# A fused macaron block: one more second product on split halves, and normalisation one chunk earlier in the loop

## The chip, the cores and the metric

The kernel runs on one core of one Trainium2 chip. The metric is device time in microseconds (us), the median of several runs of one program; a profiled execution gives the trace. The engines are TensorE (PE; its weight loads are PEld), VectorE (DVE), ScalarE (ACT), GpSimd (POOL) and SyncE (SP), which here only issues DMAs.

## What is computed

The input x is 8 x 1024 tokens of 128 values, and the program computes three steps on it:

```python
x = x + 0.5 * ffn(layernorm(x))      # phase 0
x = x + attention(layernorm(x))
x = x + 0.5 * ffn(layernorm(x))      # phase 1

def ffn(h):                          # 16 experts of 64, and one shared expert of 128
    scores = sigmoid(h @ Wg.T)       # choose 2 of 4 groups, then 4 of 16 experts, weights cw
    hid    = relu2(einsum('th,eih->eti', h, W1))          # relu2(r) = max(r, 0)**2
    out    = einsum('eth,te->th', einsum('eti,ehi->eth', hid, W2), cw)
    return out + relu2(h @ Ws1.T) @ Ws2.T
```

Attention is causal with one head of 128 and is not touched by the change.

## The kernel before

**Groups and chunks.** The 8192 tokens are 16 groups of 512 (`NG`), and each of the two feed-forward phases goes through all 16. The hidden width of 16 x 64 + 128 = 1152 is cut into nine chunks of 128 (`NCH`, chunks 0 to 8; chunk 8 is the shared expert). For each group and chunk four engines hand one 128x512 tile on:

1. PE, `up`: the first product, in three matmuls (L1189, L1190, L1191), since each fp32 operand is split into a high and a low half in the format fp32r: high x high, high x low, low x high.
2. DVE, `gate`: relu, times the square root of the routing weight (`wb`), from PSUM into `s_sb` (L939; L941 for chunk 8, which has no weight).
3. ACT, `square`: squares `s_sb` twice, once rounded into `g_hi` (L504) and once in full into `g_f` (L505). The trace calls these tiles `shared_r` and `shared`.
4. POOL, `lo_part`: `g_lo = g_f - g_hi` (L379).
5. PE, `down`: the second product, again three matmuls, accumulated over the chunks of the group.

A chunk listed in `WHOLE` goes another way: ACT makes only `g_f`, POOL does nothing, and `down` is one matmul instruction in plain fp32 with the unsplit weight `w2_f` (L1250). The trace shows two pieces for each such instruction.

**The order of work.** Nothing is scheduled automatically. Each engine has its own program, a loop body of two groups written out chunk by chunk, and semaphores between the engines. At step c of group g, PE issues `up` four chunks ahead (`AHEAD`), then what else is tied to this step, then `down(c)`. DVE, ACT and POOL also work on chunk c + 4 at step c; so at step 4 they handle chunk 8 of this group, at step 5 chunk 0 of the next one. All engines work in the order of their programs, and an instruction that waits holds those behind it.

**Normalisation.** Group g + 4 is normalised during group g:

- DVE computes statistics (L747) at steps 1 and 3 of the group before, and their mean and variance (L754, L758) at step 0.
- POOL computes the inverse root at step 1 (L398; the same instruction serves the routing weights of another group, and waits for their sum, L919).
- DVE's `norm_shift` (L778) computes the shift. Before the change this is at step 4, after the statistics of step 3, the first part of routing and the gate of chunk 8 (L941).
- ACT's `normalise` (L460) writes `xn`, four tiles of 128x128, two at step 5 and two at step 6, in each case ahead of that step's squares.
- PE transposes `xn` at step 7 (L1220), between the `up` and the `down` of that step. ACT copies the result at step 8.

Other side work: PE's `logits` (L1228) and `o_transpose` (L1262) at step 2 and `w_transpose` (L1236) at step 6; ACT's `x_hi_copy` at step 6, followed by POOL's `x_lo_part` (L385); ACT's `wT_copy` (L446, `wT`) at step 7, after which SP writes the routing weights to DRAM and reads them back spread over the partitions (L318, four DMAs into `wb`). The first two of them must have landed before chunk 0 of that group is gated, which is seven steps later.

The last two groups of a phase have no more groups to prepare. Groups 0 to 13 do, so the transposes of `xn` stand in 14 groups of each phase; the first four groups are prepared ahead of the loop.

Of the kernel before, what the change touches and what calls it, by code (L numbers as in the profile page):

```python
# [103 lines left out]
def macaron_kernel(nc, x, Qw, Kw, Vw, Wg, bias_corr, W1, W2, Ws1, Ws2, out):  # L104
# [13 lines left out]
    HB = 3  # L118
    RING = 6

    WHOLE = (1, 5)
    PREP = 4
    PR = 4
    PADT = 3 * TG
# [8 lines left out]
    with ExitStack() as ctx:  # L133
        def sb(name, shape, dt=F32):
            return ctx.enter_context(nc.sbuf_tensor(name, shape, dt))
# [14 lines left out]
        w2_lo = sb("w2_lo", [P, NCH, D], F32R)  # L150
        w2_f = sb("w2_f", [P, len(WHOLE), D])
        wgT = sb("wgT", [P, E])
# [118 lines left out]
        def wait(eng, s, value):  # L271

            if not (isinstance(value, int) and value <= 0):
                eng.wait_ge(s, value)
# [69 lines left out]
        def _(pool):  # L344
# [22 lines left out]
            def ffn(F):  # L367
# [6 lines left out]
                def lo_part(m, j):  # L374

                    if j % NCH in WHOLE:
                        return
# [67 lines left out]
        def _(sc):  # L445
# [21 lines left out]
            def ffn(F, phase):  # L467
# [26 lines left out]
                def oT_copy(g, u):  # L494
                    sc.wait_ge(F.down_done, NCH * (g + 1))
                    wait(sc, F.oTr_done, g)
                    copy(oT[:], o_ps[u]).then_inc(F.oT_copied, 1)

                def square(m, j):

                    sc.wait_ge(F.s_done, m + 1)
                    wait(sc, F.down_done, m + 1 - RING)
                    if j % NCH not in WHOLE:
                        nc.scalar.activation(g_hi[:, j % RING, :], s_sb[:, j % RING, :], ACT.Square)  # L504
# [52 lines left out]
                def body(i, first, last, extra):  # L557
                    for u in range(UN):
                        g = i * UN + u
                        for c in range(NCH):  # L560
                            j = u * NCH + c
                            if c == 0 and not (first and u == 0):
                                oT_copy(g - 1, 1 - u)
                            if c == 3 and not last:
                                sigmoid(g + 3, 1 - u, lg_ps)
                            if c in (5, 6) and not last:
                                for t in range((c - 5) * 2, (c - 5) * 2 + 2):
                                    normalise(F, g + PREP, t)
                            if c == 6 and not last:
                                x_hi_copy(g + 2, u)  # L570
                            if c == 7 and not last:
                                wT_copy(g + 2, wT_ps)
                            if c == 8 and not last:
                                x_copy(g + PREP, u, tr_ps)
                            if not (last and j + AHEAD >= UN * NCH):
                                square(i * (UN * NCH) + j + AHEAD, (j + AHEAD) % (UN * NCH))
                            extra(j)
# [100 lines left out]
            def weights_hi(w):  # L678
# [6 lines left out]
                elif w < 4:  # L685
                    for n, c in enumerate(WHOLE):
                        if c // 4 == w - 2:
# [27 lines left out]
        def _(v):  # L715
# [44 lines left out]
            def ffn(F, phase):  # L760
# [252 lines left out]
                def body(i, first, last, extra):  # L1013
                    for u in range(UN):
                        g = i * UN + u
                        for c in range(NCH):
                            j = u * NCH + c
                            m = i * (UN * NCH) + j
                            if j + AHEAD < UN * NCH:
                                gate(i, (c + AHEAD) % NCH, m + AHEAD, j + AHEAD, (j + AHEAD) // NCH)  # L1020
                            elif not last:
                                gate(i + 1, (c + AHEAD) % NCH, m + AHEAD, (j + AHEAD) % (UN * NCH), 0)
                            if not last:
                                if c == 0:
                                    mean(g + PREP)
                                if c == 1:
                                    stats(g + PREP + 1, range(2))
                                if c == 3:
                                    stats(g + PREP + 1, range(2, TG))
                                if c == 4:  # L1030
                                    norm_shift(g + PREP)

                                for part in ((7,), (8,), (), (), (9,), (), (), (), ())[c]:
                                    route(g + 2, u, part)
                                for part in ((), (), (), (0,), (1,), (2,), (3,), (4,), (5, 6))[c]:
                                    route(g + 3, 1 - u, part)
                            if c == 2 and not (first and u == 0):
                                residual(g - 1)
                            extra(j)
# [144 lines left out]
        def _(pe):  # L1184
# [30 lines left out]
            def ffn(F, phase):  # L1215
# [29 lines left out]
                def down(g, c, m, j, u):  # L1245
                    if c == 0:
                        wait(pe, F.oT_copied, g - 1)
                    if c in WHOLE:
                        pe.wait_ge(F.sq_done, m + 1)
                        mm(o_ps[u], w2_f[:, WHOLE.index(c), :], g_f[:, j % RING, :], start=(c == 0),  # L1250
                           stop=(c == NCH - 1)).then_inc(F.down_done, 1)
# [273 lines left out]
```

## Time and profile before

| | |
|---|---|
| median of 3 runs (lowest, highest) | 725.03 us (723.0, 725.87) |
| the profiled execution: its time, its span | 725.85 us, 724.1 us |
| mean granted TensorE clock | 0.982 of 2.4 GHz |
| PE, PEld busy | 685.7 us (95%), 522.5 us (72%) |
| DVE, ACT, POOL busy | 556.3 us (77%), 522.3 us (72%), 403.9 us (56%) |
| DMA | 78.37 MB, mean 108 GB/s |

The transposes of `xn` are 15.27 us apart in the group from 217.65 to 232.92, which is the length of a group in the loop. The span runs from the first to the last instruction; 1.75 us of the execution lie around it. Busy shares are means over phases of different kinds: the feed-forward phases are about 33 to 277 us and 469 to 721 us, attention lies between. Attention gives POOL almost nothing to do, so POOL's 56% says little about how full it is in the feed-forward loop. A matmul's recorded duration overlaps with the next one's, so the time that one costs PE is the distance from its start to the next start, or its piece in the chain that ended last.

### The profile page before, as it was taken

Reading aid. Unit: us, or ns where it says so; the run is one execution under the profiler, and the core shown is the slowest. Engines: PE = TensorE matmul, PEld = TensorE weight load, DVE = VectorE, ACT = ScalarE, POOL = GpSimd, SP = SyncE. Lnnn points to the kernel's source line nnn. Section 1 sums busy time; section 2 is a strip of 40 time slices with the busy share of each in tenths; the row PEclk is TensorE's granted clock in tenths of the full one; section 3 lists DMA queues with packets and bytes.
Section 4 is the critical chain, followed back from the end, with each engine's and each line's share of the span. In section 5 each row is a group of like instructions: output and inputs, shape, how many; then the busy total and the mean of one; then the engine's idle time right before and its main releaser. Section 6 shows DMA issues by size and latency. Waiting matters only on the chain.

```text
span 724.1 us, 14916 instructions
## 1 busy us (share of the span) xinstructions
PE 685.7 (95%) x3335; PEld 522.5 (72%) x3335; DVE 556.3 (77%) x2586; ACT 522.3 (72%) x1063; POOL 403.9 (56%) x314
## 2 busy tenths in 40 slices
PE   4689999999999997999999999989999999999997
PEld 3467777777777775777777777767777777777775
DVE  5978888788887885666666678978878888788863
ACT  4478788887788866675556667657888788887875
POOL 3377877778777763000000022147787777877874
PEclk9699999999999999999999999989999999999999
DMA  9766776566775650000000000554766777667772
GB/s 250 179 129 127 158 154 142 120 137 148 150 150 119 132 104 0 1 1 1 1 0 0 0 1 1 121 117 92 150 145 148 164 165 166 149 136 173 165 165 68
DMA packets 53525, 78.37 MB, mean 108 GB/s; under 512 B 5216, under 2 KB 19184, under 8 KB 53488
## 3 DMA queue, kind: packets, MB, share of 16 engines
q1 hardware_dynamic: 51280, 77.36, 49.4%
q10 hardware_dynamic: 2208, 0.59, 0.4%
q8 instruction: 14, 0.23, 0.1%
q14 instruction: 23, 0.19, 0.1%
HBM read 72.70 MB, written 5.24 MB: 108 GB/s over the span
## 4 chain that ended last, share of the span: by engine, by line
PE 49%; DVE 21%; ACT 14%; issue 12%; ACTq 1%; POOL 1%; DVEq 1%; DMA 1%; POOLq 0%
PE psum L1189 10%; PE psum L1191 10%; PE psum L1190 9%; PE psum L1398 6%; ACT shared L505 5%; ACT xn L460 4%; PE psum L1220 3%; PE psum L1250 3%; DVE nmax L1069 3%; PE psum L1228 3%; DVE s_sb L939 2%; DVE s_sb L941 2%; DVE bn L747 2%; PE psum L1387 2%; ACT shared L611 2%
## 5 line engine op out<-in xcount | busy, mean ns | idle before, releaser
L379 POOL TENSOR_TENSOR shared_r<-shared,shared_r 128x512 fp32r<-128x512 f32 x224 | 289.0, 1291 | 115.3 <-ACT shared L505 110.3
L939 DVE SCALAR_TENSOR_TENSOR s_sb<-psum,wb 128x512 f32<-128x512 f32 x256 | 176.2, 690 | 75.8 <-PE psum L1191 65.6
L504 ACT ACTIVATE shared_r<-s_sb 128x512 fp32r<-128x512 f32 x224 | 141.3, 631 | 83.0 <-DVE s_sb L939 74.4
L505 ACT ACTIVATE shared<-s_sb 128x512 f32<-128x512 f32 x288 | 178.3, 620 | 21.7 <-DVE s_sb L939 21.4
L1189 PE MATMUL psum<-x_hi,w_hi 128*128 128x512 f32 x288 | 139.3, 484 | 2.7 <-DVE x_sb L1095 2.3
L1191 PE MATMUL psum<-x_hi,w_lo 128*128 128x512 f32 x288 | 115.3, 401 | 0.0
L1190 PE MATMUL psum<-x_lo,w_hi 128*128 128x512 f32 x288 | 114.5, 397 | 0.0
L1189 PE MATMUL psum<-shared_r,w_hi 128*128 128x512 f32 x224 | 97.8, 437 | 0.6 <-POOL shared_r L379 0.4
L1190 PE MATMUL psum<-shared_r,w_hi 128*128 128x512 f32 x224 | 89.2, 398 | 0.0
L1191 PE MATMUL psum<-shared_r,w_lo 128*128 128x512 f32 x224 | 89.0, 398 | 0.0
L362 POOL TENSOR_TENSOR a_rstd<-a_mv,neg_half 128x8 f32<-128x8 f32 x8 | 13.1, 1637 | 116.5 <-DVE a_mv L758 116.5
L1189 PEld LDWEIGHTS psum<-x_hi,w_hi 128*128 128x128 f32 x288 | 55.1, 191 | 29.6 <-issue 11.7
L1190 PEld LDWEIGHTS psum<-x_lo,w_hi 128*128 128x128 f32 x288 | 54.9, 191 | 23.9 <-issue 14.1
L1250 PE MATMUL psum<-shared,w_f 128*128 128x512 f32 x128 | 65.3, 592 | 0.0
L611 ACT ACTIVATE shared<-psum,nmax 128x128 f32<-128x128 f32 (+3 forms) x64 | 47.5, 743 | 23.6 <-DVE nmax L1069 22.3
L1191 PEld LDWEIGHTS psum<-x_hi,w_lo 128*128 128x128 f32 x288 | 54.8, 190 | 12.8
L1069 DVE TENSOR_REDUCE nmax<-psum 128x1 f32<-128x128 f32 (+3 forms) x64 | 47.6, 753 | 19.6 <-PE psum L1378 19.5
L460 ACT ACTIVATE xn<-x_sb,shift,roots 128x128 f32 (+1 forms) x128 | 55.7, 484 | 3.0 <-DVE shift L778 3.0
L1189 PEld LDWEIGHTS psum<-shared_r,w_hi 128*128 128x128 f32 x224 | 42.8, 191 | 11.0 <-POOL shared_r L379 2.4
L1191 PEld LDWEIGHTS psum<-shared_r,w_lo 128*128 128x128 f32 x224 | 42.5, 190 | 10.1
L398 POOL TENSOR_TENSOR roots<-powers,neg_half 128x8 f32<-128x8 f32 x28 | 45.9, 1638 | 6.6 <-issue 5.2
L1190 PEld LDWEIGHTS psum<-shared_r,w_hi 128*128 128x128 f32 x224 | 42.9, 192 | 6.5 <-issue 0.4
(166 smaller groups left out, 1312.1 us busy)
## 6 DMA issues: line engine op xcount, KB each, us to landing
wb<-scratch SPq DMA_DIRECT2D x128, 512.0 KB, 8.4
out<-x_sb SPq DMA_DIRECT2D x16, 256.0 KB, 9.8
x_sb<-in_L_attn_x SPq DMA_DIRECT2D x4, 256.0 KB, 6.2
scratch<-wT SPq DMA_DIRECT2D x32, 32.0 KB, 1.9
w_raw<-in_L_ffn_W ACTq DMA_DIRECT2D x1, 512.0 KB, 5.8
w_raw<-in_L_ffn_W SPq DMA_DIRECT2D x1, 512.0 KB, 6.4
w_raw<-in_L_ffn_Ws ACTq DMA_DIRECT2D x1, 64.0 KB, 8.6
w_raw<-in_L_ffn_Ws SPq DMA_DIRECT2D x1, 64.0 KB, 6.9
```

Source lines behind the costliest of these rows:

```text
L379: nc.gpsimd.tensor_tensor(g_lo[:, j % RING, :], g_f[:, j % RING, :], g_hi[:, j % RING, :].bitcast(F32), ALU.subtract).then_inc(F.glo_done, 1)
L398: nc.gpsimd.tensor_tensor(roots[:], powers[:], neg_half[:, 0:2 * TG], ALU.pow).then_inc(F.rstd_done, 1)
L460: ins = nc.scalar.activation(xn[:, t, :], x_sb[:, bass.ds(g * TG + t, 1), :].rearrange("p t d -> p (t d)"), ACT.Identity, bias=shift[:, t: ...
L504: nc.scalar.activation(g_hi[:, j % RING, :], s_sb[:, j % RING, :], ACT.Square)
L505: nc.scalar.activation(g_f[:, j % RING, :], s_sb[:, j % RING, :], ACT.Square).then_inc(F.sq_done, 1)
L611: nc.scalar.activation(prob[:, t % PR, 0:w], sc_ps[t % 2][:, 0:w], ACT.Exp, bias=nmax[:, u, t:t + 1], accum_out=rsum[:, u, t:t + 1]).then_ ...
L939: ins = nc.vector.scalar_tensor_tensor(s_, h_, 0.0, wb[:, u, c, :], ALU.max, ALU.mult)
L1069: nc.vector.tensor_reduce(nmax[:, u, t:t + 1], sc_ps[t % 2][:, 0:(t + 1) * P], AX.X, ALU.max, negate=True).then_inc(A.max_done, 1)
L1189: mm(out_, l_hi, r_hi, start=start, stop=False)
L1190: mm(out_, l_hi, r_lo, start=False, stop=False)
L1191: return mm(out_, l_lo, r_hi, start=False, stop=stop)
L1250: mm(o_ps[u], w2_f[:, WHOLE.index(c), :], g_f[:, j % RING, :], start=(c == 0), stop=(c == NCH - 1)).then_inc(F.down_done, 1)
```

## The change

Two things are changed. `WHOLE` loses chunk 1, so that only chunk 5 takes the plain fp32 way. And DVE's `norm_shift` moves from step 4 to the end of the statistics in step 3, and ACT's four normalisations from steps 5 and 6 to steps 4 and 5.

```diff
-    WHOLE = (1, 5)
+    WHOLE = (5,)
...
-                            if c in (5, 6) and not last:
-                                for t in range((c - 5) * 2, (c - 5) * 2 + 2):
+                            if c in (4, 5) and not last:
+                                for t in range((c - 4) * 2, (c - 4) * 2 + 2):
                                     normalise(F, g + PREP, t)
                             if c == 6 and not last:
                                 x_hi_copy(g + 2, u)
...
                                 if c == 3:
                                     stats(g + PREP + 1, range(2, TG))
-                                if c == 4:
                                     norm_shift(g + PREP)
```

On ACT, steps 4 to 7 of a group before the change: squares of chunk 8 (L504 and L505), two normalisations, squares of chunk 0 of the next group, two normalisations, the copy `x_hi`, the one square of chunk 1, and the copy `wT`.

```order
L504 ACTIVATE shared_r<-s_sb 128x512
L505 ACTIVATE shared<-s_sb 128x512
L460 ACTIVATE xn<-x_sb,shift,roots 128x128 x2
L504 ACTIVATE shared_r<-s_sb 128x512
L505 ACTIVATE shared<-s_sb 128x512
L460 ACTIVATE xn<-x_sb,shift,roots 128x128 x2
L446 ACTIVATE x_hi<-x_f 128x512
L505 ACTIVATE shared<-s_sb 128x512
L446 ACTIVATE wT<-psum 64x128
```

The same steps of the changed kernel:

```order
L460 ACTIVATE xn<-x_sb,shift,roots 128x128 x2
L504 ACTIVATE shared_r<-s_sb 128x512
L505 ACTIVATE shared<-s_sb 128x512
L460 ACTIVATE xn<-x_sb,shift,roots 128x128 x2
L504 ACTIVATE shared_r<-s_sb 128x512
L505 ACTIVATE shared<-s_sb 128x512
L446 ACTIVATE x_hi<-x_f 128x512
L504 ACTIVATE shared_r<-s_sb 128x512
L505 ACTIVATE shared<-s_sb 128x512
L446 ACTIVATE wT<-psum 64x128
```

Each pair of normalisations has moved ahead of one pair of squares, and chunk 1 has two squares instead of one, ahead of the copy `wT`.

On DVE, steps 3 and 4 (statistics, the shift, the first two operations of routing, the gate of chunk 8, the weights `scw`), as a difference:

```order
 L747 BN_STATS bn<-x_sb 128x6 x2
+L778 SCALAR_TENSOR_TENSOR shift<-psum,roots 128x4
 L836 TENSOR_TENSOR psum<-scores,psum 128x64
 L837 TENSOR_SCALAR psum<-scores 128x64
 L941 TENSOR_SCALAR s_sb<-psum 128x512
-L778 SCALAR_TENSOR_TENSOR shift<-psum,roots 128x4
 L927 SCALAR_TENSOR_TENSOR scw<-psum,roots 128x4x16
```

The shift now stands ahead of the gate of chunk 8, and with it its wait for POOL's inverse root. POOL gets one more subtraction (L379) in each of the 32 groups, behind `x_lo` (L385) of step 6. PE has three matmuls with split halves in place of one plain one at `down(1)`. Nothing else moves.

## Rows read from the trace of the kernel before

**Rows 1.** The page: span, and busy time of each engine.

```profile
span 724.1 us, 14916 instructions
PE 685.7 (95%) x3335; PEld 522.5 (72%) x3335; DVE 556.3 (77%) x2586; ACT 522.3 (72%) x1063; POOL 403.9 (56%) x314
```

**Rows 2.** Windows: one group of phase 0 (stretch, length, busy us, clock, DMA share, GB/s).

```profile
202.50:217.70 15.20, 14.94 (x70) 11.53 (x71) 12.57 (x65) 12.41 (x26) 12.07 (x10) 1.00 0.65 140
```

**Rows 3.** Timeline of PE around transposes (start, duration, [idle before, releaser]).

```profile
49.11 1.04 PE L1220 MATMUL psum<-ident,xn 128*128 128x128 f32 x4 [1.88 <-ACT xn L460]
65.78 0.63 PE L1220 MATMUL psum<-ident,xn 128*128 128x128 f32 x4 [0.18 <-ACT xn L460]
...
217.04 0.40 PE L1191 MATMUL psum<-x_hi,w_lo 128*128 128x512 f32 x1
217.65 0.63 PE L1220 MATMUL psum<-ident,xn 128*128 128x128 f32 x4 [0.21 <-ACT xn L460]
...
232.92 0.63 PE L1220 MATMUL psum<-ident,xn 128*128 128x128 f32 x4 [0.37 <-ACT xn L460]
...
692.00 0.63 PE L1220 MATMUL psum<-ident,xn 128*128 128x128 f32 x4 [0.18 <-ACT xn L460]
```

**Rows 4.** The chain that ended last, at `down(1)`: start, its piece.

```profile
207.13 0.23 PE psum L1191
207.36 0.86 PE psum L1250 x2
```

**Rows 5.** Groups of instructions: the plain and the split second product.

```profile
L1250 PE MATMUL psum<-shared,w_f 128*128 128x512 f32 x128 | 65.3, 592 | 0.0
L1189 PE MATMUL psum<-shared_r,w_hi 128*128 128x512 f32 x224 | 97.8, 437 | 0.6 <-POOL shared_r L379 0.4
L1190 PE MATMUL psum<-shared_r,w_hi 128*128 128x512 f32 x224 | 89.2, 398 | 0.0
L1191 PE MATMUL psum<-shared_r,w_lo 128*128 128x512 f32 x224 | 89.0, 398 | 0.0
```

**Rows 6.** Timeline of ACT, steps 3 to 7 of one group.

```profile
212.89 0.62 ACT L505 ACTIVATE shared<-s_sb 128x512 f32<-128x512 f32 x1
...
214.81 0.87 ACT L460 ACTIVATE xn<-x_sb,shift,roots 128x128 f32 x2
215.59 0.62 ACT L504 ACTIVATE shared_r<-s_sb 128x512 fp32r<-128x512 f32 x1
...
216.63 0.88 ACT L460 ACTIVATE xn<-x_sb,shift,roots 128x128 f32 x2
...
217.92 0.63 ACT L505 ACTIVATE shared<-s_sb 128x512 f32<-128x512 f32 x1
218.44 0.27 ACT L446 ACTIVATE wT<-psum 64x128 f32<-64x128 f32 x1
```

**Rows 7.** Timeline of DVE: statistics of step 3 in the same group.

```profile
212.24 0.48 DVE L747 BATCH_NORM_STATS2 bn<-x_sb 128x6 f32 x2
```

**Rows 8.** Timeline of POOL: the inverse root, and `x_lo`, in the same group.

```profile
209.56 1.64 POOL L398 TENSOR_TENSOR roots<-powers,neg_half 128x8 f32<-128x8 f32 x1
...
218.10 1.30 POOL L385 TENSOR_TENSOR x_lo<-x_f,x_hi 128x512 fp32r<-128x512 f32 x1
```

**Rows 9.** Timeline of PE: `down(1)` of the following group.

```profile
222.31 0.59 PE L1250 MATMUL psum<-shared,w_f 128*128 128x512 f32 x1
```

**Rows 10.** L914 by line (ns min/median/max), then DVE's and POOL's timelines near 479 us.

```profile
L914 DVE SCALAR_TENSOR_TENSOR chosen<-marked,scores x32: 218/218/1299, 17.1 to 682.3; 128x64 f32<-128x64 f32 x32
...
479.50 1.30 DVE L914 SCALAR_TENSOR_TENSOR chosen<-marked,scores 128x64 f32<-128x64 f32 x1
...
478.20 2.51 POOL L379 TENSOR_TENSOR shared_r<-shared,shared_r 128x512 fp32r<-128x512 f32 x2 [1.09 <-ACT shared L505]
```

**Rows 11.** The weight loads begun at 220.9 and 221.7, and DVE's gate of chunk 0.

```profile
DMA to landing us min/median/max: 5.3/6.6/7.9
...
229.81 0.69 DVE L939 SCALAR_TENSOR_TENSOR s_sb<-psum,wb 128x512 f32<-128x512 f32 x1
```

## The prediction, on record before the changed kernel ran

> **What bounds the kernel now.** I read the page's busy shares first: PE 95%, the others 56 to 77% [rows 1]. That is not yet an argument, since a mean over phases of different kinds hides where an engine is full. The windows over one group of a feed-forward phase say more: of 15.20 us PE is busy 14.94, DVE 12.57, ACT 12.41, POOL 12.07, at full clock [rows 2]. So PE is the bound in this loop, each other engine has 2.6 to 3.1 us to spare per group, and what shortens or lengthens PE's own sequence moves the end. The timeline of PE shows where it loses its 0.26 us and a bit more: once per group, ahead of the transposes of `xn`, and the releaser is ACT's normalisation [rows 3]. Last I read the three other engines' timelines over one group, to see what is early and what is late at each hand-over.
>
> How long is that stall? Matmuls follow each other every 0.23 us here [rows 4]. The last one before the transposes started at 217.04, so they could have started at 217.27; they started at 217.65, 0.38 us late. The view's idle time, 0.21, leaves out the tail of the last matmul, 0.17 us. With that added the stalls alternate between about 0.36 (0.18 or 0.21 shown) and 0.54 (0.37 shown) through 27 groups, from 65.78 to 692.00. Their mean is 0.45 us. The 28th, in group 0 of phase 0, is 1.88 + 0.17 = 2.05 us, and the transposes behind it take 1.04 us instead of 0.63: the granted clock fell from its upper to its lower level there [rows 3].
>
> **The stall, step by step.** ACT's squares of chunk 7 start at 212.89 (the second one), the first pair of normalisations only at 214.81, behind the squares of chunk 8, and the second pair at 216.63, behind those of chunk 0 [rows 6]. From the starts: a square costs ACT 0.52 us (217.92 to 218.44), a pair of normalisations 0.78 (214.81 to 215.59), both squares of a chunk 1.04 (215.59 to 216.63), and `x_hi` what is left of 217.92 - 216.63, 0.51. In the changed order the first pair can start when the square of chunk 7 is through, at 212.89 + 0.52 = 213.41, if its shift is there. The shift needs POOL's root, done at 209.56 + 1.64 = 211.20 [rows 8], and DVE's statistics, done at 212.24 + 0.48 = 212.72 [rows 7]: it is there at about 212.9. Then ACT runs without a gap: first pair to 214.19, squares of chunk 8 to 215.23, second pair to 216.01. PE wants `xn` at 217.27. The stall is gone with 1.2 us to spare. Saved: 27 x 0.45 = 12.1 us.
>
> In group 0 of phase 0 the second pair moves ahead of one pair of squares, 1.04 us, while 2.05 are lost: I count 1.0 us saved. Bounds: 0, if the shift is late there, and 2.05 plus about 1 us for the slow clock behind it (an estimate; a transpose group alone loses 0.4 of it), if the gap becomes short enough that the clock stays up.
>
> **The product of chunk 1.** In the chain the plain fp32 matmul takes 0.86 us of PE, a matmul of a split product 0.23 [rows 4], so three take 0.70: 0.16 us less, in 32 groups 5.1. In the two groups 0 PE also waits for others right behind, so I count 30: 4.8 us. One could come out on the other side. By busy time a plain product costs 65.3 / 64 = 1.02 us and a split one (97.8 + 89.2 + 89.0) / 224 = 1.23 [rows 5], so that the edit would cost 0.21 x 32 = 6.7 us instead. I go by the chain, because these durations overlap: 398 ns on record, but a start every 233 ns. The Trainium skill (Perfetto Trace Analysis, section Identifying the Most-Contended Engine) calls matmul busy time a poor measure for just this reason; by its other measure, the share of weight loads, the edit would look like a cost as well, three loads for two. The rows allow the test, since the two numbers differ in sign.
>
> **What it adds elsewhere.** One square on ACT, 0.52 us, and one subtraction on POOL, 1.30 us by the row of `x_lo`, which is the same operation of the same size [rows 8]. The group from 217.65 to 232.92 took 15.27 us [rows 3]; without its stall of 0.54 that is 14.73, with the cheaper product 14.57 us for every group. In these ACT has 12.41 + 0.52 = 12.9 and POOL 12.07 + 1.30 = 13.4 us of work. Both fit, POOL with 1.2 us left, so what hides them is PE's own work, and no longer by much. What matters is whether they are late at a hand-over. ACT, continued from 216.01: squares of chunk 0 to 217.05, `x_hi` to 217.57, squares of chunk 1 to 218.61, then `wT`, which began at 218.44 before. POOL: the subtraction for chunk 0 from about 217.2 to 218.5, `x_lo` to 219.8, the new one for chunk 1 to 221.1. PE asks for it at `down(1)`, 222.31 before [rows 9], 221.93 without the stall. It is 0.8 us early. The ones behind it (chunks 2 to 4) end at 222.4, 223.7 and 225.0 and are wanted two to three us later, since PE does the logits and other transposes first. I take 0 for waits there; the bounds are 0 and 0.2 us per group, the rest by which my stacking of starts may be wrong, 5.4 us in all.
>
> The moved shift waits for POOL's root ahead of the gate of chunk 8. With POOL's backlog the root ends at about 211.6 in place of 211.2; the shift is due at 212.7 less what PE gained before, 212.1. No wait; if one came, the gate behind it, and ACT's squares behind that, have a few tenths before ACT is free for them anyway. Price 0.
>
> **Sum.** Against the profiled execution, 725.85 us: 12.1 + 4.8 + 1.0 = 17.9 less, 707.9. That execution lies 0.8 us above the median of the runs shown, 725.03, so the median should be **707.1 us**.
>
> **Rivals.**
>
> 1. *Weight loads take the place of the stall* (still faster). The load that gates chunk 0 landed at 221.7 + 7.9 = 229.6, and the gate began at 229.81 [rows 11]. After the change the gate is wanted 0.54 earlier, at 229.27, and `wT`, which starts the load, comes 0.2 later. DVE will wait there in some groups. For: the circle from `wT` to the landing (229.6 - 218.44 = 11.2), the gate (0.69), 1.04 of squares, 0.51 for `x_hi` and 1.04 of squares again is 14.5 us, just PE's new 14.57. Against: a gate wanted at 229.27 would end at 229.96, and ACT, busy normalising until 216.01 + 14.57 = 230.58, asks for it 0.6 us later. If all loads took 0.4 us longer than this one, the period would be 14.9 and 27 x 0.35 = 9 us lost: 716. Chance 9%.
> 2. *The stall stays* (the change doesn't do what it says), because ACT is held up as much by its extra square and a late shift as it gains. Then only the products gain: 720. Against it stand the 1.2 us. Chance 5%.
> 3. *POOL holds DVE.* DVE's L914 reads two SBUF tiles and took 1.30 us at 479.50, beside two subtractions in a row from 478.20 [rows 10], where its median is 0.22. With POOL running back to back after step 7, L914 (once per group, at about 223.0) will fall into a subtraction and wait up to 1.3 us, 0.7 on average. A gate is asked for only when PE wants its PSUM buffer again, three chunks later, and a chunk is six matmuls of 0.23, 1.4 us; 4.2 less the gate's own 0.69 leaves room, so I price it at 0; were it all passed on, 28 x 0.7 = 20 us would be lost: 727, no change. The Trainium skill (GPSIMD Engine Reference, section Specifications) states that GpSimd shares its SBUF interfaces with VectorE and contends with instructions of two SBUF inputs; by that rule this rival's wait will be seen, and the row at 479.50 agrees. Chance that it decides: 4%.
> 4. *Slower: the new subtraction comes late at `down(1)`.* It stands third in POOL's queue behind chunk 0 and `x_lo`. PE would wait each group. The gain per group is 0.61 us, so it decides from 0.8 + 0.61 = 1.4 us later than my 221.1, at 222.5. At 1.6 us late, 28 x 0.2 = 5.6 us are lost: 731. For: POOL's 13.4 of 14.57 us, where a queue forms easily. Against: the queue starts from an idle POOL in each group, since 1.2 us are left. Chance 4%.
>
> The forecast itself gets 78%.
>
> **How the numbers follow.** A measurement of this kernel tells about 0.5%, 3.6 us, from no change. The forecast's own range: at the low end 12.1 + 5.1 + 3.1 saved, 704.7; at the high end 0.2 us of new waits in 27 groups, 712.5. With a part of rival 1 the range is 704.2 to 714. Faster by over 0.5%: forecast, rivals 1 and 2, 92%. Within 0.5%: rival 3, 4%. Slower: rival 4, 4%.
>
> **What would show it.** In the changed trace: no idle time before L1220 released by ACT in 27 groups; distances between transposes of 14.5 to 14.7 us where one was 15.27; three matmuls 0.23 us apart at `down(1)`; ACT 12.9 and POOL 13.4 us busy in a group; no PE wait for POOL's L379 in the loop; L914 longer in most groups and gates of chunk 0 released by a DMA in some, with PE not following. It would be wrong if PE idles per group somewhere new, at `down(1)` above all, or if PE's own pace with more fp32r matmuls isn't 0.23 us.

## The result and the profile after

| | median (lowest to highest, runs) | profiled execution, span |
|---|---|---|
| before | 724.38 us (723.0 to 725.87, 4) | 725.85 us, 724.1 us |
| changed | 702.89 us (702.53 to 702.95, 4) | 702.95 us, 701.2 us |

The ratio is 0.970, 95% interval 0.969 to 0.971: the change saves 21.5 us. I had forecast 707.1 and a range from 704.2 to 714.0, so the result lies 1.3 us below the range's low end.

The page of the changed kernel, span and busy times, which answers to [rows 1]:

```profile
span 701.2 us, 15091 instructions
PE 673.3 (96%) x3367; PEld 527.5 (75%) x3367; DVE 567.5 (81%) x2586; ACT 529.6 (76%) x1094; POOL 438.2 (62%) x346
```

The windows over one group of phase 0, with the columns of [rows 2]:

```profile
208.67:223.22 14.55, 14.55 (x71) 11.70 (x70) 12.67 (x64) 12.55 (x27) 13.01 (x10) 1.00 0.68 148
```

PE is now busy for the whole of the group, and POOL has 13.0 us of work in it. By the page POOL has 34.3 us more than before, 1.07 us for each of the 32 groups.

The timeline of PE around transposes, for [rows 3] (lines of the program are one lower than before from L1031 on: L1188 to L1190 are the three matmuls, L1219 is the transpose, L1249 the plain product, L1094 the attention's last step on DVE):

```profile
48.26 0.63 PE L1219 MATMUL psum<-ident,xn 128*128 128x128 f32 x4 [0.82 <-ACT xn L460]
...
208.67 0.60 PE L1219 MATMUL psum<-ident,xn 128*128 128x128 f32 x4
...
222.99 0.39 PE L1190 MATMUL psum<-x_hi,w_lo 128*128 128x512 f32 x1
223.22 0.60 PE L1219 MATMUL psum<-ident,xn 128*128 128x128 f32 x4
...
669.42 0.60 PE L1219 MATMUL psum<-ident,xn 128*128 128x128 f32 x4
```

The last matmul starts at 222.99 and the transposes 0.23 us later: no gap is left. Nor is there one ahead of the transposes in any other of the 27 groups.

One group of phase 1, from 654.58 to 669.42, took 14.84 us where the others took 14.55 or 14.56. DVE, POOL and PE in it:

```profile
653.50 0.69 DVE L939 SCALAR_TENSOR_TENSOR s_sb<-psum,wb 128x512 f32<-128x512 f32 x1 [1.54 <-DMA wb<-scratch]
...
658.05 5.04 POOL L379 TENSOR_TENSOR shared_r<-shared,shared_r 128x512 fp32r<-128x512 f32 x4
...
659.40 0.50 PE L1188 MATMUL psum<-shared_r,w_hi 128*128 128x512 f32 x1
```

The gate of chunk 0 waited 1.54 us for its weights, so the new subtraction, the first of the four, ended only at 658.05 + 1.26 = 659.31. `down(1)`, due at 658.98 + 0.23 = 659.21, started 0.2 us late. A wait for the weights of this length still reaches PE, by way of POOL.

The chain that ended last, at `down(1)`, for [rows 4]:

```profile
213.46 0.23 PE psum L1188
213.70 0.23 PE psum L1189
213.93 0.23 PE psum L1190
```

Groups of instructions, the first matmul of the split product and the plain one, for [rows 5]; PE's only idle time before the split products is 0.8 us in the whole program:

```profile
L1188 PE MATMUL psum<-shared_r,w_hi 128*128 128x512 f32 x256 | 109.5, 428 | 0.8 <-POOL shared_r L379 0.7
L1249 PE MATMUL psum<-shared,w_f 128*128 128x512 f32 x64 | 32.6, 592 | 0.0
```

The timelines of ACT and POOL in the same group, for [rows 6] and [rows 8]:

```profile
206.75 0.86 ACT L460 ACTIVATE xn<-x_sb,shift,roots 128x128 f32 x2
...
211.24 5.04 POOL L379 TENSOR_TENSOR shared_r<-shared,shared_r 128x512 fp32r<-128x512 f32 x4
```

ACT's second pair ends at 206.75 + 0.86 = 207.61, 1.06 us before PE wants it (I had 1.2). POOL's first subtraction in the row of four is the new one: it ends at 211.24 + 1.26 = 212.50, and `down(1)` starts at 213.30, 0.8 us later, as forecast.

L914 by line, for [rows 10]:

```profile
L914 DVE SCALAR_TENSOR_TENSOR chosen<-marked,scores x32: 217/713/1205, 17.1 to 660.4; 128x64 f32<-128x64 f32 x32
```

DVE's gate of chunk 0 in this group, for [rows 11]; it waits for a DMA, and PE has no gap behind it:

```profile
221.18 0.69 DVE L939 SCALAR_TENSOR_TENSOR s_sb<-psum,wb 128x512 f32<-128x512 f32 x1 [0.59 <-DMA wb<-scratch]
```

**Where the 22.9 us between the two profiled executions came from.** The distances between the same transposes of `xn` in both traces give it stretch by stretch (those of phase 1's first four groups stand inside attention):

| stretch | before | changed | saved | forecast |
|---|---|---|---|---|
| start to group 0's transposes, phase 0 | 49.11 | 48.26 | 0.85 | 1.0 |
| to the next transposes | 16.67 | 14.87 | 1.80 | 0.5 |
| 12 groups of phase 0's loop | 182.22 | 174.64 | 7.58 | 7.3 |
| phase 0's last transposes to phase 1's first ones (end of phase 0, most of attention) | 173.90 | 174.75 | -0.85 | 0.3 |
| from there to phase 1's fourth ones (end of attention) | 53.01 | 52.99 | 0.0 | 0 |
| group 0 of phase 1 | 19.89 | 14.43 | 5.46 | 0.4 |
| 13 groups of phase 1's loop | 197.20 | 189.48 | 7.72 | 7.9 |
| the rest | 32.1 | 31.8 | 0.3 | 0.3 |

(The forecast column is worked out from the prediction's terms: 0.45 + 0.16 us a group in the loop, the 1.0 us of group 0, the stalls of 0.36 and 0.43 us at the transposes that end the second and the sixth stretch, and 0.16 for each product outside.) The loop is right to within 0.3 us in each phase. Three single places are not, above all the first group of phase 1.

**The first group of phase 1, before and after.** The timelines of DVE and PE in the kernel before, near 479 us:

```profile
478.54 1.04 DVE L913 SCALAR_TENSOR_TENSOR rt_sb<-marked,rt_sb 128x64 f32<-128x64 f32 x1
479.50 1.30 DVE L914 SCALAR_TENSOR_TENSOR chosen<-marked,scores 128x64 f32<-128x64 f32 x1
481.00 1.26 DVE L1095 SCALAR_TENSOR_TENSOR x_sb<-psum,rinv,x_sb 128x128 f32<-128x128 f32 x4
482.31 0.51 PE L1189 MATMUL psum<-x_hi,w_hi 128*128 128x512 f32 x1 [2.27 <-DVE x_sb L1095]
```

and the windows over what follows:

```profile
482.30:489.50 7.20, 7.18 (x22) 5.99 (x23) 3.42 (x12) 4.08 (x7) 2.92 (x2) 0.53 0.60 117
```

The row at 479.50 is the one that I had in hand as a warning [rows 10]. I did not follow it to PE. POOL's two subtractions from 478.20 to 480.7 hold L913 and L914 for 0.8 and 1.1 us, the attention's last step L1095 stands behind them, and PE stands idle 2.27 us for it. After that gap the granted clock is 0.53 of 2.4 GHz over 7.2 us, so most of the time at its lower level of 1.2 GHz. The same place in the changed kernel, DVE, POOL and PE:

```profile
464.00 1.30 DVE L897 SCALAR_TENSOR_TENSOR rt_sb<-rt_sb,inv_u 128x64 f32<-128x64 f32 x1
469.14 0.23 DVE L913 SCALAR_TENSOR_TENSOR rt_sb<-marked,rt_sb 128x64 f32<-128x64 f32 x1
469.28 0.22 DVE L914 SCALAR_TENSOR_TENSOR chosen<-marked,scores 128x64 f32<-128x64 f32 x1
...
463.95 1.27 POOL L379 TENSOR_TENSOR shared_r<-shared,shared_r 128x512 fp32r<-128x512 f32 x1 [0.46 <-ACT shared L505]
...
469.49 2.53 POOL L379 TENSOR_TENSOR shared_r<-shared,shared_r 128x512 fp32r<-128x512 f32 x2 [0.73 <-ACT shared L505]
...
471.02 0.50 PE L1188 MATMUL psum<-x_hi,w_hi 128*128 128x512 f32 x1 [0.52 <-DVE x_sb L1094]
```

The new subtraction for chunk 1 (463.95) holds DVE earlier, at L897, where there is room. Counted from the transposes of `xn` at 474.91 before and 465.51 after, the gate and the squares behind it come 1.1 us later and POOL's pair 0.7 us later, while L913 keeps its place, so that L913 and L914 now run just ahead of that pair. PE waits 0.52 us, and the clock stays up. The 5.46 us are 1.75 of wait, 0.16 of product, 0.43 of wait at `xn`, and what is left, some 3.1, goes with the clock.

### The profile page after: what moved, and what is told of

Its sections match the earlier page's. It is cut to its first block, busy times and chain, and to the rows that moved or that the text cites. A ratio compares the mean times of both kernels' runs of the same rounds, so it can differ in the third digit from the quotient of the medians.

```text
span 701.2 us, 15091 instructions
## 1 busy us (share of the span) xinstructions
PE 673.3 (96%) x3367; PEld 527.5 (75%) x3367; DVE 567.5 (81%) x2586; ACT 529.6 (76%) x1094; POOL 438.2 (62%) x346
## 4 chain that ended last, share of the span: by engine, by line
PE 78%; DVE 10%; ACT 5%; issue 3%; POOL 1%; DMA 1%; POOLq 0%; DVEq 0%; ACTq 0%
PE psum L1188 18%; PE psum L1190 18%; PE psum L1189 18%; PE psum L1397 7%; PE psum L1227 4%; PE psum L1249 4%; DVE nmax L1068 3%; PE psum L1219 2%; PE psum L1261 2%; PE psum L1386 2%; ACT shared L611 2%; PE psum L1410 2%; DVE zn L1082 1%; DVE s_sb L939 1%; ACT wb L446 1%
## 5 line engine op out<-in xcount | busy, mean ns | idle before, releaser
L379 POOL TENSOR_TENSOR shared_r<-shared,shared_r 128x512 fp32r<-128x512 f32 x256 | 325.9, 1294 | 55.6 <-ACT shared L505 53.5
L505 ACT ACTIVATE shared<-s_sb 128x512 f32<-128x512 f32 x288 | 178.1, 620 | 28.6 <-DVE s_sb L939 28.6
L504 ACT ACTIVATE shared_r<-s_sb 128x512 fp32r<-128x512 f32 x256 | 159.8, 624 | 45.3 <-DVE s_sb L939 43.5
L1188 PE MATMUL psum<-x_hi,w_hi 128*128 128x512 f32 x288 | 127.2, 442 | 1.0 <-DVE x_sb L1094 0.5
L1190 PE MATMUL psum<-x_hi,w_lo 128*128 128x512 f32 x288 | 114.3, 397 | 0.0
L1188 PE MATMUL psum<-shared_r,w_hi 128*128 128x512 f32 x256 | 109.5, 428 | 0.8 <-POOL shared_r L379 0.7
L1189 PE MATMUL psum<-shared_r,w_hi 128*128 128x512 f32 x256 | 101.2, 395 | 0.0
L1190 PE MATMUL psum<-shared_r,w_lo 128*128 128x512 f32 x256 | 101.0, 395 | 0.0
L1188 PEld LDWEIGHTS psum<-x_hi,w_hi 128*128 128x128 f32 x288 | 54.5, 189 | 21.6 <-issue 7.2
L1190 PEld LDWEIGHTS psum<-x_hi,w_lo 128*128 128x128 f32 x288 | 54.2, 188 | 12.9
L1188 PEld LDWEIGHTS psum<-shared_r,w_hi 128*128 128x128 f32 x256 | 48.2, 188 | 13.6 <-POOL shared_r L379 3.8
L1190 PEld LDWEIGHTS psum<-shared_r,w_lo 128*128 128x128 f32 x256 | 48.1, 188 | 11.3
L1189 PEld LDWEIGHTS psum<-shared_r,w_hi 128*128 128x128 f32 x256 | 48.5, 189 | 7.7 <-issue 0.2
L1397 PE MATMUL psum<-wb,zn 128*128 128x512 f32 (+3 forms) x128 | 47.2, 513 | 0.0
```

Of the source, the lines that this page charges most:

```text
L379: nc.gpsimd.tensor_tensor(g_lo[:, j % RING, :], g_f[:, j % RING, :], g_hi[:, j % RING, :].bitcast(F32), ALU.subtract).then_inc(F.glo_done, 1)
L505: nc.scalar.activation(g_f[:, j % RING, :], s_sb[:, j % RING, :], ACT.Square).then_inc(F.sq_done, 1)
L1188: mm(out_, l_hi, r_hi, start=start, stop=False)
L1189: mm(out_, l_hi, r_lo, start=False, stop=False)
L1190: return mm(out_, l_lo, r_hi, start=False, stop=stop)
L1397: ins = mm(u_ps[:, q0:], zn[:, u, k, :], pT[half][:, k, q0:], start=(k == 0), stop=(k == last - 1))
```

## The experiments

The theory: the moved normalisation takes 27 stalls of 0.45 us, the product 0.16 us a group, and the rest of the gain is an accident of the positions of POOL's subtractions against DVE's operations on two SBUF tiles. The rival: the moved normalisation mended the first group of phase 1 too, or the split product isn't cheaper and something else gives the whole. All ratios are to the kernel before.

### One part at a time

```diff
--- before
-    WHOLE = (1, 5)
+    WHOLE = (5,)
```

> The kernel before with the first part of the change alone: chunk 1's second product on split halves, normalisation left in iterations 5 and 6. My theory: chunk 1's product saves 0.16 us in each of 32 groups (5.1), the idle time of 0.45 us before the transposes stays in 27 groups, and the start of phase 1 loses its 2.3 us wait and the half-clock stretch behind it, since the additional subtraction of the opening chunks moves POOL's later pair away from DVE's routing instructions (4.9): 724.4 - 5.1 - 4.9 = 714.4 us. Rival: the start of phase 1 was mended by the moved normalisation and not by chunk 1: 719.3 us. Second rival: the stall at the transposes grows by ACT's 0.52 us in every group, so that the product gains nothing: 724 us or above.

```diff
--- changed
-    WHOLE = (5,)
+    WHOLE = (1, 5)
```

> The changed kernel with chunk 1's product put back on the plain operands, so that only the normalisation is moved. My theory: the 27 stalls of 0.45 us go (12.1), group 0 of phase 0 gains about 1 to 2, and the first group of phase 1 stays at some 19.5 us with its wait of about 2.3 us for DVE and a half clock behind it: 724.4 - 13.6 = 710.8 us. Rival: the moved normalisation is what mended the start of phase 1 too: 706 us.

Measured with only the product changed: 722.23 us (719.8 to 724.1, 9 runs), 0.995 (0.993 to 0.997). With only the normalisation moved: 709.13 us (709.0 to 710.8), 0.979 (0.977 to 0.981).

The second run is near the expectation. The transposes are 14.70 or 14.71 us apart in every group of both loops, without a gap, which is the changed kernel's 14.55 plus 0.16. The first group of phase 1 keeps its wait of 2.24 us and takes 17.9 us; the windows behind it show the lower clock for a shorter time (0.67 over 5.1 us). So the moved normalisation alone does not mend that group.

By the medians the two parts alone save 2.2 and 15.3 us, 4 us less than the 21.5 of both together.

The first run misses all three expectations, 714.4, 719.3 and 724. Its first group of phase 1 did fall from 19.89 to 16.00 us, by chunk 1 alone, with the clock at its upper level throughout; a wait of 1.39 us for ACT's `xn` is left in it (490.47), which the moved normalisation takes away in the changed kernel's 14.43. But its loops gained nothing: the 12 groups of phase 0 took 182.26 us where 182.22 stood before, and the 13 of phase 1 took 199.0 where 197.2 stood. About half of the groups took 14.90 to 15.11 us, the others up to 16.21. One of these, on DVE, ACT and PE:

```profile
92.62 0.69 DVE L939 SCALAR_TENSOR_TENSOR s_sb<-psum,wb 128x512 f32<-128x512 f32 x1 [1.25 <-DMA wb<-scratch]
...
91.55 0.86 ACT L460 ACTIVATE xn<-x_sb,shift,roots 128x128 f32 x2
93.34 0.63 ACT L504 ACTIVATE shared_r<-s_sb 128x512 fp32r<-128x512 f32 x1 [0.93 <-DVE s_sb L939]
93.88 0.61 ACT L505 ACTIVATE shared<-s_sb 128x512 f32<-128x512 f32 x1
94.40 0.86 ACT L460 ACTIVATE xn<-x_sb,shift,roots 128x128 f32 x2
...
95.41 0.63 PE L1220 MATMUL psum<-ident,xn 128*128 128x128 f32 x4 [1.23 <-ACT xn L460]
```

The gate of chunk 0 waits 1.25 us for its weights' DMA. ACT has nothing wrong with its own work, but the squares of chunk 0 are next in its program, so it waits with DVE, and the second pair of normalisations, which needs neither, waits behind them. PE then waits 1.23 us. In the other groups the same lengths stand together, DMA wait and PE wait: 0.93 and 0.88, 0.63 and 0.59, 0.88 and 0.86, 0.96 and 1.11. The longest wait, 1.48 us at 643.09, belongs to them too, though the view names PE:

```profile
640.22 0.69 DVE L939 SCALAR_TENSOR_TENSOR s_sb<-psum,wb 128x512 f32<-128x512 f32 x1 [1.36 <-PE psum L1191]
...
643.09 0.63 PE L1220 MATMUL psum<-ident,xn 128*128 128x128 f32 x4 [1.48 <-ACT xn L460]
```

PE's product for that gate was done at 638.14 + 0.40 = 638.54. The second of its two DMAs, issued at 631.5, landed 8.5 us later at 640.0, 0.2 us before the gate. I did not follow the waits of 0.47 to 0.62 us in phase 1 one by one.

This makes a new theory: what the moved normalisation brings is more than 0.45 us a group. It takes `xn` out of the line behind the gate weights' DMA.

### Only the second pair of normalisations ahead of the square that waits

```diff
--- before, with WHOLE = (5,)
-                            if c in (5, 6) and not last:
-                                for t in range((c - 5) * 2, (c - 5) * 2 + 2):
+                            if c == 5 and not last:
+                                for t in range(TG):
```

> The kernel before with chunk 1's product on split halves, and of the moved normalisation only one thing: ACT's second pair of normalisations goes from iteration 6 to iteration 5, ahead of the square of the next group's chunk 0; the first pair and the shift stay where they were. My theory: chunk 1's product alone gave 2.8 us where 5 to 10 were expected because that square waits for a gate that waits for the gate weights' transfer, and the second pair stood behind it in ACT's queue; with the pair ahead of it no transposes wait at all and the loop runs at 14.55 us a group as after the change: 27 groups by 0.6 us, 707 us or a little below, with group 0 of phase 0 keeping most of its 1.9 us wait. Rival: what made the loop with the split product uneven is the load of ACT and POOL itself (the squares and subtractions), not the order: some 718 to 722 us as in that run.

Measured: 704.36 us (703.8 to 704.9), 0.972 (0.971 to 0.974). By the medians that is 17.9 us less than the run with the product alone (16.4 by the two ratios), and no work was taken away: one pair of instructions stands ahead of two others on one engine. The same group, on DVE, ACT and PE:

```profile
90.35 0.69 DVE L939 SCALAR_TENSOR_TENSOR s_sb<-psum,wb 128x512 f32<-128x512 f32 x1 [0.74 <-DMA wb<-scratch]
...
89.80 1.64 ACT L460 ACTIVATE xn<-x_sb,shift,roots 128x128 f32 x4
91.34 0.61 ACT L504 ACTIVATE shared_r<-s_sb 128x512 fp32r<-128x512 f32 x1
...
92.26 0.60 PE L1220 MATMUL psum<-ident,xn 128*128 128x128 f32 x4
```

The DMA is still late, by 15.9 us in 15 waits over the whole program, against 11.5 in 12 with the product alone, and PE's waits for ACT's `xn` are 4.5 us in 3 (opening and group 0) against 20.3 in 30. The late DMA no longer reaches PE through `xn`; once in the loops, behind a DMA wait of 1.98 us, it reaches PE through POOL's subtraction, as 0.34 us at 645.39, and that group took 15.17 us. This settles the order as the cause. The median is 2.6 us under the 707 that I expected. I had expected group 0 of phase 0 to keep its wait of 1.9 us; it fell to 0.83, as after the change, and in this trace no slow clock followed. What the earlier shift and the earlier first pair add to this is at most the 1.5 us to 702.9, and the intervals don't separate it from nothing.

### Work taken away, and work added, in the first group of phase 1

The first kernel is the changed one, where in phase 1 the very first chunk 1 stays plain (POOL's count for chunk 0 goes up by two in its place):

```diff
--- changed
+    whole = lambda F, m, c: c in WHOLE or (F is FF[1] and isinstance(m, int) and m == 1)
...
-                    if j % NCH in WHOLE:
+                    if whole(F, m, j % NCH):
                         return
```

> The changed kernel, but in phase 1 the very first chunk 1 (group 0) keeps its plain product: one ACT square of 0.6 us and one POOL subtraction of 1.3 us fewer in the whole program. My theory: POOL is then early again by one subtraction, its pair of later subtractions lies on top of DVE's two routing instructions L913 and L914, TensorE waits some 2 us and then runs at half clock for several us: 702.9 + 5 = 707.9 us, from work taken away. Rival: the gain at the start of phase 1 has another cause (the moved normalisation): 703.0 us, no change against the changed kernel beyond the 0.16 us of the product.

The second is the kernel before, with one square and one subtraction in the same place whose results no product uses:

```diff
--- before
+                    extra = F is FF[1] and isinstance(m, int) and m == 1
-                    if j % NCH in WHOLE:
+                    if j % NCH in WHOLE and not extra:
                         return
...
+                        if phase == 1 and isinstance(m, int) and m == 1:
+                            pe.wait_ge(F.more_done, 1)
```

> The kernel before, all products and the normalisation as they were, with work added that serves nothing: in phase 1's group 0 ACT also makes the rounded square of chunk 1 and POOL also subtracts for it; TensorE still multiplies the plain operands, and waits for that subtraction first. My theory: the added 1.3 us on POOL holds DVE earlier, where there is room, and moves the later pair off L913 and L914: the wait of 2.3 us before the first group's transposes of the attention's end goes, with the half clock: 724.4 - 4.9 + 0.2 = 719.7 us, faster by adding work. Rival: without the other parts of the change the added work is worth nothing or costs its 0.6 to 1.3 us: 724.4 to 725.7 us.

Measured: 705.91 us (704.3 to 708.9), 0.975 (0.972 to 0.977), for the first, 3.0 us slower than the changed kernel by doing less, where the theory said 5. 720.67 us (720.2 to 722.6) for the second, 0.994 (0.992 to 0.996), some 4 us faster than the kernel before by doing more, near the 719.7 expected. Lines are two higher in both (L915 and L916 are L913 and L914). In the first one, on DVE and PE:

```profile
469.05 1.03 DVE L915 SCALAR_TENSOR_TENSOR rt_sb<-marked,rt_sb 128x64 f32<-128x64 f32 x1
470.00 1.30 DVE L916 SCALAR_TENSOR_TENSOR chosen<-marked,scores 128x64 f32<-128x64 f32 x1
...
472.82 0.50 PE L1190 MATMUL psum<-x_hi,w_hi 128*128 128x512 f32 x1 [2.26 <-DVE x_sb L1096]
```

the windows behind that wait:

```profile
472.80:480.00 7.20, 7.18 (x33) 5.70 (x34) 5.53 (x23) 5.88 (x11) 4.28 (x3) 1.00 0.61 120
```

and in the second kernel, on DVE and PE:

```profile
478.50 0.23 DVE L915 SCALAR_TENSOR_TENSOR rt_sb<-marked,rt_sb 128x64 f32<-128x64 f32 x1
478.64 0.22 DVE L916 SCALAR_TENSOR_TENSOR chosen<-marked,scores 128x64 f32<-128x64 f32 x1
...
480.38 0.50 PE L1191 MATMUL psum<-x_hi,w_hi 128*128 128x512 f32 x1 [0.35 <-DVE x_sb L1097]
...
490.86 0.63 PE L1222 MATMUL psum<-ident,xn 128*128 128x128 f32 x4 [1.38 <-ACT xn L462]
```

The wait of 2.26 us comes back with one subtraction fewer, and goes with one more. So the place of POOL's pair is the cause of that wait. In the second kernel, whose normalisation is not moved, 1.1 us of it turns up again at `xn` (1.38 against 0.26 before); what makes that group 3.9 us shorter (15.99 against 19.89) is mostly the clock, which stayed at its upper level. The clock is a separate matter. In the first kernel's profiled execution (704.62 us) it stayed at 1.00 behind the same wait where it was 0.53 before, and that group took 16.34 us against 19.89. The six runs of this kernel spread over 4.7 us, more than the 3.1 us that went with the fall before. I have no trace of the long ones, so that a fall is what divides them was not shown.

### All nine products split

```diff
--- changed
-    WHOLE = (5,)
+    WHOLE = ()
```

> The changed kernel with the last plain product, chunk 5's, on split halves too: one more square of 0.52 us on ACT and one more subtraction of 1.26 us on POOL per group. TensorE would need 14.55 - 0.16 = 14.39 us a group (697.8 us in all). My theory: POOL then has ten subtractions and the powers, 10 x 1.27 + 1.64 = 14.34 us, in a loop of 14.39, with no slack for waiting on ACT and DVE, so POOL sets the pace: between 14.6 and 15.1 us a group, 704 to 720 us, slower than the changed kernel. Rival: it still fits: 698 us.

Then with chunk 5's subtraction on DVE in place of POOL:

```diff
+                            if c == 3:
+                                v.wait_ge(F.sq_done, m + 3)
+                                tt(g_lo[:, (j + 2) % RING, :], g_f[:, (j + 2) % RING, :], f32(g_hi[:, (j + 2) % RING, :]),
+                                   ALU.subtract).then_inc(F.glo5_done, 1)
```

> The changed kernel with all nine second products on split halves, but chunk 5's subtraction on DVE (behind the gate of chunk 7) and not on POOL. ACT makes one square more per group. TensorE needs 14.39 us a group, POOL keeps its 13.0 us, DVE goes from 12.7 to 13.4. My theory: with POOL left as it was, its limit (14.37 of 14.37 us busy with all nine) is gone and TensorE's pace holds: 29 groups by 0.16 us under the changed kernel, 697.9 us, with the subtraction on DVE at 0.7 to 2.0 us, since it reads two SBUF tiles and is held while a POOL operation runs. Rival: that hold delays the next gate, and with it ACT's squares and the products: 703 us or more.

Measured: 710.9 us (708.9 to 711.9), 0.981 (0.979 to 0.983), with POOL doing all nine: 8.0 us slower than the changed kernel. And 702.08 us (700.1 to 702.9) with DVE's help, beside 702.66 for the changed kernel in the same set. The windows over one group of the first:

```profile
199.01:213.38 14.37, 14.37 (x72) 11.83 (x71) 12.14 (x60) 13.55 (x28) 14.37 (x12) 1.00 0.60 125
```

PE's timeline in the group before that one:

```profile
196.00 0.50 PE L1188 MATMUL psum<-shared_r,w_hi 128*128 128x512 f32 x1 [1.07 <-POOL shared_r L379]
```

and the windows over one group of the second:

```profile
191.98:206.35 14.37, 14.37 (x72) 11.81 (x71) 13.37 (x69) 13.59 (x29) 13.36 (x11) 1.00 0.68 143
```

With nine subtractions on POOL the time lies in the expected range of 704 to 720 us. In the group of the first windows POOL is busy 14.37 of 14.37 us. Such groups mostly alternate with groups of 15.7 us in phase 0 (in phase 1 they are milder), and PE waits 15 times for POOL, 11.8 us in all. But POOL is not simply full in the long groups. The one from 183.28 to 199.01, on DVE and POOL:

```profile
189.07 2.31 DVE L914 SCALAR_TENSOR_TENSOR chosen<-marked,scores 128x64 f32<-128x64 f32 x1
...
186.25 5.05 POOL L379 TENSOR_TENSOR shared_r<-shared,shared_r 128x512 fp32r<-128x512 f32 x4
193.07 1.64 POOL L398 TENSOR_TENSOR roots<-powers,neg_half 128x8 f32<-128x8 f32 x1 [1.78 <-DVE powers L919]
```

POOL's row of four holds L914 until the last of them ends (191.30), over 2.31 us. L919, the sum that POOL's root needs, stands behind it, so POOL then waits 1.78 us for DVE, and PE 1.07 us for POOL. In all eight groups of both loops in which L914 took over 2 us POOL stood idle 1.5 to 2.0 us ahead of its root, and these groups have PE's eight long waits, 8.7 of the 11.8 us. That is rival 3 of the prediction, come true one step further on. One more step along the way that this change took thus makes it slower.

With the ninth on DVE all groups are 14.36 to 14.40 us in phase 0, as expected (in phase 1 up to 14.62), and the two-SBUF subtraction took 0.68 us in 27 groups and 1.1 to 1.7 in 5. The median still fell short of 697.9 and of a clear gain: the intervals of this kernel (0.967 to 0.972) and of the changed one overlap. Its profiled execution took 700.14 us; 1.64 of the 2.2 us missing there are the end of phase 0, which took 176.39 us against 174.75. Why the median is another 1.9 us longer was not traced.

### The end of phase 0

Between phase 0's last transposes and phase 1's first ones the changed kernel lost 0.85 us. POOL's four subtractions in a row from 250.78 lie on DVE's `zn` of the attention. DVE in the changed kernel, and PE behind it:

```profile
252.20 3.98 DVE L1082 TENSOR_SCALAR zn<-x_sb,a_mv,a_rstd 128x128 f32<-128x128 f32 x4
...
258.51 0.66 PE L1261 MATMUL psum<-ident,oT 128*128 128x128 f32 x4 [0.70 <-ACT oT L446]
```

Before, the same four operations took 2.82 us, with two of the four held by a subtraction (1.08 and 1.31 us) and two at 0.33 us; after, three are held. Two kernels leave chunk 1 (the first), or chunks 1 and 5 (the second, built on the one with DVE's help) plain in phase 0's last group only:

```diff
+    whole = lambda F, m, c: c in WHOLE or (F is FF[0] and isinstance(m, int) and m == (NG - 1) * NCH + 1)
```

> The changed kernel, but in the very last group of phase 0 chunk 1 keeps its plain product. My theory: the change lost 0.85 to 1.1 us between phase 0's last group and the attention, because that subtraction makes POOL run four in a row while DVE writes zn; without it this is won back: 702.9 - 0.9 = 702.0 us. Rival: the loss is elsewhere: 703.0 us.

> The changed kernel with a plain product in chunk 1 of phase 0's last group, a second time, beside the changed kernel. My theory: 0.9 us under it, 702.0 us, in the executions whose loop is undisturbed. Rival: the earlier median of 702.3 was chance, and it equals the changed kernel: 702.9 us.

> The changed kernel once more, as the comparison for the other two on the same chip: 702.9 us by both theories.

> The run with chunk 5's subtraction on DVE, with plain products in chunks 1 and 5 of phase 0's last group, so that POOL and DVE are freed of one subtraction each just before the attention starts. In that run the stretch from phase 0's last transposes of xn to the attention's transposes took 176.4 us against 173.9 where POOL had no such subtraction. My theory: the stretch falls back to some 174 us, worth 2.2 us after the 0.3 us of the two plain products: 702.1 - 2.2 = 699.9 us in the median, 697.9 in the best executions. Rival: the loss there was DVE's additional square-root and routing work and not those subtractions: 702 us.

Measured: 702.26 us (701.2 to 703.6) and, repeated, 701.91 us (701.5 to 702.5) beside 702.66 (702.5 to 703.4) for the changed kernel. The ratios' intervals overlap, but the stretch itself took 173.86 and 173.87 us in the two traces, and 174.75 and 174.88 in the changed kernel's two: 0.9 to 1.0 us, as expected. DVE's `zn` took 2.98 us in the repeated one. The combination gave **699.35 us** (699.1 to 701.5), 0.966 (0.964 to 0.968), the best of all, against 702.66 and 0.970 (0.968 to 0.973) for the changed kernel; its stretch took 173.95 us.

## Why the prediction was right, and where it was wrong

- *27 stalls of 0.45 us, 12.1 us.* Right. None is left, and with the normalisation alone moved the groups are 14.71 us.
- *The product of chunk 1, 0.16 us by the chain.* Right, and the busy times, which said +0.21 us, were wrong in sign: 14.71 less 14.55 us in every group. The Trainium skill's warning about matmul busy time (Perfetto Trace Analysis, Identifying the Most-Contended Engine) holds here. Its other measure, the weight loads' share, rose from 72% to 75% while the time fell; read as a cost, as I read it in the prediction, it had the wrong sign.
- *ACT and POOL on time.* Right: 0.8 us early at `down(1)`, and late once in the two loops, by 0.2 us behind a DMA wait of 1.54 us. The prices were near: I had ACT 12.9 and POOL 13.4 us in a group, 12.6 and 13.0 were measured.
- *Group 0 of phase 0, 1.0 us.* The wait fell by 1.06 us as reckoned. The step behind it, from 16.67 to 14.87 us, gave 1.8 where I had 0.5: the slow clock, which I had as a bound and not as the value, was not there. That the shorter wait is why is not shown. The clock stayed up in all nine traces with a wait of 0.59 to 0.83 us there; with 1.87 to 1.88 us it fell in two (before, and with the added work) and stayed up in the third, the product alone, where this step took 14.94 us. So some 1.3 us of the 22.9 may be the luck of one execution.
- *"In the two groups 0 PE also waits for others right behind, so I count 30."* This is the step that failed. Group 0 of phase 1 gave 5.46 us. I had given it 0.4, because I held what PE waits for there to be untouched by the change. It was DVE, held by POOL, and the change moves POOL. With chunk 1's product alone 3.9 of the 5.46 us are there; the other 1.6 are the wait at `xn` that the moved normalisation takes away. Some 3.1 of them are the clock, which after such a wait fell fully in the trace before, for half as long in the run with the normalisation alone, and not at all in the run with one plain chunk 1.
- *The end of phase 0* cost 0.85 us where I had 0.3 saved, for the same reason with the other sign.

The three together, 1.3 + 5.0 - 1.2 = 5.1 us, are what lies between the sum's 707.9 and the profiled 702.95, within 0.2. The range failed because its low end held only the clock of one group 0. The gain of group 0 of phase 1 is luck: nothing in the change aims at it. The experiment that puts this accident back gave 705.9, inside the range.

- *Rival 1, weight loads.* It did not decide, but it was the right thing to fear. DVE's gates wait for that DMA 14.7 us in 21 waits in the changed kernel, longest 2.8. In the order before, with PE at its faster product, the same waits went on to PE and ate the whole gain. I had priced the moved normalisation as 0.45 us of stall and did not see that it also takes `xn` out of that line.
- *Rival 3, POOL holds DVE.* The hold is there: L914's median went from 0.22 to 0.71 us. PE doesn't follow in the loop, until all nine products are split: then L914 takes up to 2.98 us and PE follows. The Trainium skill (GPSIMD Engine Reference, Specifications) says that GpSimd and VectorE instructions with two SBUF inputs contend for SBUF; the traces agree, with 0.22 us for L914 alone and 1.30 us at 479.50.

## What to carry to other kernels

Read every long wait of the bound engine to its first cause, the ones that happen once as well: a wait of 2.3 us was worth 3.0 us in the medians when it was put back, and 5 us between two traces with the slow clock behind it, and it hung on the position of a neighbour's operation. In an engine's program, put work that depends on nothing late ahead of work that waits for a DMA; here one such swap was worth 16 to 18 us without any work removed. And when one engine takes over work group by group, stop while it still has slack: POOL at 13.0 of 14.55 us was hidden, with one more subtraction it cost 8 us, because its unbroken row held DVE, and POOL then waited for DVE.

## What the runs showed of the hardware

- DVE operations on two SBUF tiles end with a POOL subtraction that they meet (L897 at 465.30, POOL's subtraction at 465.22). 64 values per partition took 0.22 us alone and up to 1.30 us beside subtractions of 1.27 us in the kernel before. In a row of subtractions DVE can lose to the next ones too: up to 2.98 us with all nine split. The same kind of instruction with one operand in PSUM (L913 in the loop, 29 times) took 0.23 us each time.
- Not every POOL operation holds DVE: 27 of DVE's own subtractions began during POOL's inverse root (1.64 us, 8 values per partition) and took 0.68 us.
- An operation on one SBUF tile can be held too: one `zn` of 128 values took 0.33 us alone and 1.08 to 1.35 us where it began under one of POOL's subtractions; four took 1.1 us with POOL idle, 2.82 in the kernel before and 3.98 in the changed one.
- After a wait of the same length (2.24 to 2.27 us) in the same place, the granted clock was 0.53 over 7.2 us, 0.67 over 5.1 us, or did not fall at all. The same holds for the 1.87 to 1.88 us ahead of group 0 of phase 0: it fell in two traces of three.
- A plain fp32 matmul of 512 columns costs PE 0.16 us more than three fp32r ones (0.86 against 3 x 0.233 us).
